# Decays repeated four tiles at a time, row terms of stage 4 beside its values, and another order of turns

## What is computed

```python
x = _layernorm(x + _L0_attn_ref(x, ...))   # stage 0: state space mixer and MLP
x = _layernorm(x + _L0_ffn_ref(x, ...))    # stage 1: attention and experts
x = _layernorm(x + _L1_attn_ref(x, ...))   # stage 2: linear attention
x = _layernorm(x + _L1_ffn_ref(x, ...))    # stage 3: binarized MLP
x = _layernorm(x + _L2_attn_ref(x, ...))   # stage 4: attention, 16 heads, full width
x = _layernorm(x + _L2_ffn_ref(x, ...))    # stage 5: experts
x = _layernorm(x + _L3_attn_ref(x, ...))   # stage 6: attention with pruning
x = _layernorm(x + _L3_ffn_ref(x, ...))    # stage 7: experts
```

```python
delta = softplus(dt @ dt_proj_w.T + dt_proj_b)
dA = exp(delta * A)                       # per token, feature and state
dBu = delta * Bm * u
h = dA_t * h + dBu_t                      # over the 256 tokens; y = sum over states of h * C
```

## Time and profile before

| | before |
|---|---|
| median of 3 runs | 1339.96 us |
| profiled execution: time, span | 1339.95, 1338.2 us |
| mean granted clock of TensorE | 0.978 |
| busy: TensorE, its weight loads | 96%, 68% |
| busy: VectorE, ScalarE, GpSimd | 69%, 68%, 57% |
| chain that ended last: TensorE | 82% |

### The profile page before, as it was taken

How to read it: one execution, slowest core, us unless ns; L and a number is a source line. 1 busy time by engine, 2 the same in 40 slices (tenths; PEclk the granted TensorE clock), 3 DMA queues, 4 the chain that set the end, 5 groups by cost and what they waited for, 6 DMA issues and landing times.

```text
span 1338.2 us, 26178 instructions
## 1 busy us (share of the span) xinstructions
PE 1285.8 (96%) x8764; PEld 910.6 (68%) x8764; DVE 922.5 (69%) x3611; ACT 909.0 (68%) x2503; POOL 768.9 (57%) x845
## 2 busy tenths in 40 slices
PE   8999789999998999999999999999999999999997
PEld 4445356567754777678777777777788877876665
DVE  5777998868757677757566454797597678764244
ACT  6667899777585789675868565557577758755221
POOL 2878877568539477476665755447534525442525
PEclk9679999999998999999999999999999999999999
DMA  8744000110042000102000101201200021004230
GB/s 291 190 127 108 1 2 1 57 57 2 1 142 85 1 2 2 57 24 104 4 1 1 64 1 38 92 1 64 83 2 1 2 80 17 2 1 135 55 103 24
DMA packets 23109, 67.87 MB, mean 51 GB/s; under 512 B 2336, under 2 KB 9120, under 8 KB 20672
## 3 DMA queue, kind: packets, MB, share of 16 engines
q1 hardware_dynamic: 22976, 66.20, 15.6%
HBM read 62.85 MB, written 3.34 MB: 49 GB/s over the span
## 4 chain that ended last, share of the span: by engine, by line
PE 82%; ACT 6%; POOL 5%; DVE 5%; issue 1%; DMA 1%; SPq 0%; POOLq 0%; DVEq 0%; ACTq 0%
PE bank L1193 71%; PE bank L1197 11%; ACT arena L1651 3%; POOL arena L2461 1%; ACT L1651 1%; POOL arena L2465 1%; DVE arena L1912 1%; ACT bank L1651 1%; DVE stats L1926 1%; DVE stats L1915 1%; POOL arena L2524 1%; POOL stats L2452 0%; DVE arena L2091 0%; POOL arena L2474 0%; DVE stats L1929 0%
## 5 line engine op out<-in xcount | busy, mean ns | idle before, releaser
L1651 ACT ACTIVATE arena<-arena 128x256 f32<-128x256 f32 (+4 forms) x804 | 355.8, 446 | 50.1 <-POOL arena L2517 26.5
L1651 ACT ACTIVATE arena<-bank 128x512 f32<-128x512 f32 (+2 forms) x347 | 183.8, 560 | 204.4 <-PE bank L1193 135.1
L1193 PE MATMUL bank<-XT,W 128*128 128x512 f32 (+1 forms) x752 | 293.3, 525 | 0.0
L2474 POOL TENSOR_TENSOR arena<-arena 128x512 f32<-128x512 f32 (+1 forms) x108 | 170.6, 1595 | 153.4 <-DVE arena L1912 50.0
L1193 PEld LDWEIGHTS bank<-W,arena 128*128 128x128 f32 x1888 | 227.9, 192 | 39.2 <-issue 32.0
L1193 PE MATMUL bank<-W,arena 128*128 128x128 f32 x1888 | 238.2, 276 | 1.3 <-DVE arena L2173 0.8
L1193 PE MATMUL bank<-arena 128*32 128x256 f32 (+8 forms) x2912 | 225.5, 334 | 9.8 <-POOL arena L2484 2.7
L2523 POOL TENSOR_TENSOR arena<-arena 128x256 f32<-128x256 f32 x192 | 119.2, 621 | 189.2 <-DVE arena L2163 188.9
L1193 PEld LDWEIGHTS bank<-arena 128*32 128x32 f32 (+4 forms) x2912 | 152.8, 152 | 83.4 <-issue 48.2
L2524 POOL TENSOR_TENSOR arena<-arena 128x512 f32<-128x512 f32 x192 | 201.5, 1049 | 0.0
L1197 PE MATMUL bank<-CF,arena 128*128 128x128 f32 x1312 | 184.0, 277 | 12.0 <-POOL arena L2524 5.3
(11 more groups left out here) (143 smaller groups left out, 1670.2 us busy)
## 6 DMA issues: line engine op xcount, KB each, us to landing
arena<-rws SPq DMA_DIRECT2D x8, 2048.0 KB, 7.5
arena<-rep SPq DMA_DIRECT2D x62, 256.0 KB, 5.3
arena<-rws SPq DMA_DIRECT2D x4, 1792.0 KB, 6.4
W<-w SPq DMA_DIRECT2D x2, 2124.0 KB, 8.2
arena<-rws SPq DMA_DIRECT2D x8, 384.0 KB, 10.1
W<-w SPq DMA_DIRECT2D x1, 2692.0 KB, 9.5
XT<-wkq SPq DMA_DIRECT2D x4, 512.0 KB, 6.0
W<-w SPq DMA_DIRECT2D x1, 2005.0 KB, 15.7
```

The lines of the kernel that those rows point to most:

```text
L1193: return e.matmul(o, lhsT, rhs, start=start, stop=stop, skip_group_check=True)
L1651: return e.activation(o, a, func, **kw)
L2474: e.tensor_tensor(h, h, w, ALU.mult).then_inc(has["gw"], 1)
```

## The change

1. Decays: "0.da" takes four tiles at a time, into banks A, B, C and D, in all four row strips of TensorE. A bank is held until the scan of its tile. The four exponentials of a group follow in one step each, and the condition on the scan of two tiles before is gone.
2. Row terms: the step "4.r" is gone. A new step "4.c" on VectorE copies the row matrix behind the value weights (a place "rk" of 16 columns, loaded as zeros with the weights), so that "4.v" makes values and row terms in one matmul of 144 columns per token tile. It takes two banks, with two tiles each, and VectorE reads values and row terms from both.
3. Costs and turns: the planner's costs are changed in many places (for the load "er" 6.5 in place of 9.0 us, for "ew" 1.5 in place of 2.0), and TURNS is new as a whole. Chunk 1 comes before chunk 0 in stage 0, where chunk 0 came first.

```diff
@@ places and operands
-    [("wv", 128), ("bv", 1), ("wp", 128), ("bp", 128)],
+    [("wv", 128), ("rk", 16), ("bv", 1), ("wp", 128), ("bp", 128)],
-W_AT = {3: WMAX - 1160, 2: WMAX, 4: 4135}
+W_AT = {3: WMAX - 1160, 2: WMAX, 4: 4119}
+        def values4():
+            return W[0][:, W_AT[4]:W_AT[4] + 144]
@@ banks and conditions of the decays
-for _q in range(16):
-    if _q % 2 == 0:
-        HELD["0.da", _q] = [("A", 0, ("0.st", _q, 0), 1, 1), ("B", 0, ("0.st", _q + 1, 0), 1, 1)]
+for _q in range(0, 16, 4):
+    HELD["0.da", _q] = [("ABCD"[_k], 0, ("0.st", _q + _k, 0), 1, 1) for _k in range(4)]
-            if q % 2:
+            if q % 4:
                 add("0.da", q, ("0.da", q - 1))
             else:
-                add("0.da", q, ("0.dc", 0), ("0.a", 0, PREP), *([("0.st", q - 2)] if q >= 2 else []))
+                add("0.da", q, ("0.dc", 0), ("0.a", 0, PREP))
@@ TensorE, 0.da
-                    two = [uses["AB"[k] if name == "0.da" else "bc"[k], name, c, n] for k in range(2)]
-                    for b in two:
+                    some = [uses[k, name, c, n] for k in ("ABCD" if name == "0.da" else "bc")]
+                    for b in some:
                         on.wait_ge(*free(b))
-                    for k, b in enumerate(two):
+                    for k, b in enumerate(some):
                         r, w = slice(32 * (n % 4 + k), 32 * (n % 4 + k) + 32), n // 4 * 128
...
@@ TensorE, 4.v and 4.r
-                    b, ps = first(name, c)
-                    for j in range(4):
-                        ins = mm(ps[:, j * 128:(j + 1) * 128], cols_(4, c)[:, j * 128:(j + 1) * 128], wt(4, "wv"))
-                    ins.then_inc(full[b.i], 1)
+                    on.wait_ge(*after("rk", "4.c", PREP))
+                    for k, (b, ps) in enumerate((first(name, c), second(name, c))):
+                        for j in range(2):
+                            js = slice((2 * k + j) * 128, (2 * k + j + 1) * 128)
+                            ins = mm(ps[:, j * 144:(j + 1) * 144], cols_(4, c)[:, js], values4())
+                        ins.then_inc(full[b.i], 1)
-                elif name == "4.r":
-                    b, ps = first(name, c)
...
-                    for j in range(4):
-                        ins = mm(ps[:, j * 16:(j + 1) * 16], cols_(4, c)[:, j * 128:(j + 1) * 128], pre[:, 48:64])
-                    ins.then_inc(full[b.i], 1)
@@ VectorE, 4.c and 4.v
+                elif name == "4.c":
...
+                    e.tensor_copy(wt(4, "rk"), pre[:, 48:64]).then_inc(has["rk"], 1)
...
+                    for k in range(2):
+                        b = u("bc"[k], name, c)
+                        on.wait_ge(*filled(b))
+                        for j in range(2):
+                            e.tensor_copy(values_in(4, c, 2 * k + j), values_from(bank[b.i][:, 144 * j:144 * j + 128], 0))
+                        tt(row4(c)[:, 32 * k:32 * k + 32].rearrange("p (i h) -> p i h", i=2),
+                           bank[b.i][:, 0:288].rearrange("p (i x) -> p i x", i=2)[:, :, 128:144],
+                           pre[:, 64:80].unsqueeze(1).to_broadcast([128, 2, 16]), ALU.add).then_inc(done[b.i], 1)
```

More of the change, by code:

```diff
@@ L174, in emits @@
     if name == "0.da":
-        return {"dA": (1 - n % 2, 1)}
+        return {"dA": (n % 4 == 0, 1)}
     return EMITS.get(name, {})
@@ L180, in parts_of @@
     t = PARTS[name]
-    t = t[n % 2] if isinstance(t, tuple) else t
+    t = t[n % len(t)] if isinstance(t, tuple) else t
     both = [x.split("|") for x in t.split()]
@@ L311, in stage_steps @@
         add("4.vz")
-        add("4.v", 0, ("4.vz", 0))
-        add("4.r", 0, ("load", 0, PREP, 4))
+        add("4.v", 0, ("4.vz", 0), ("4.c", 0, PREP))
         for i in range(16):
             add("4.qk", i, ("load", 0, PREP, 4), *([("4.ex", last_reader(i - 5))] if i >= 5 else []))
-        attention(lambda u: [("4.r", 0)] + [("4.qk", u // 2 * 4 + k) for k in range(4)], lambda u: [("4.v", 0)])
+        attention(lambda u: [("4.v", 0)] + [("4.qk", u // 2 * 4 + k) for k in range(4)], lambda u: [("4.v", 0)])
         add("4.y", 0, *[("4.pv", u) for u in range(UNITS)])
@@ L359, in weight_steps @@
     return loads + [("0.a", 0, 0, []), ("0.f", 0, 0, []), ("0.w", 0, 0, []), ("3.p", 3, 0, [("1.n", 0, 0, 1)]), ("3.p", 3, 1, [("3.p", 0)]), ("6.a", 6, 0, [("load", 0)])] + [
-        ("1.a", 1, 0, [("0.dt", 0, 0, 0)]), ("3.b", 3, 0, [("1.n", 0, 0, 1)]), ("4.b", 4, 0, [("load", 0)]), ("6.b2", 6, 0, [("load", 0)])]
+        ("1.a", 1, 0, [("0.dt", 0, 0, 0)]), ("3.b", 3, 0, [("1.n", 0, 0, 1)]), ("4.b", 4, 0, [("load", 0)]), ("4.c", 4, 0, [("load", 0)]), ("6.b2", 6, 0, [("load", 0)])]
 TASKS = [[(s, 0) for s in range(8)], [(s, 1) for s in range(8)],
@@ L369 @@
 TURNS = {
[33 rows of a table removed]
-        1352), ("0.e", 0, 3): (1356, 1362, 1366, 1370), ("0.w", 0, PREP): (5,), ("0.f", 0, PREP): (7, 11), ("0.a", 0, PREP): (8,
-        21, 23), ("4.l", 0, PREP): (65, 94, 224, 202), ("4.k", 0, PREP): (114,), ("4.a", 0, PREP): (136, 159, 119, 128, 257, 269,
-        222, 232), ("4.g", 0, PREP): (178, 184, 147, 171, 284, 297, 237, 252), ("4.st", 0, PREP): (194, 186, 343, 301), ("1.n", 1,
[50 rows of a table removed]
-        1841, 1847, 1850, 1855), ("1.a", 1, PREP): (81, 86, 87), ("2.t", 2, 0): (983, 988, 993, 989, 994, 1007, 1034, 1041, 1046,
[22 rows of a table removed]
-        2046, 2049, 2052, 2056), ("3.p", 3, PREP): (387, 404, 413, 420, 432, 439, 448, 489), ("3.b", 3, PREP): (416, 417), ("4.r",
[47 rows of a table removed]
-        (2553, 2556, 2559, 2560, 2562), ("load", 4, PREP): (1252,), ("4.b", 4, PREP): (1313, 1363), ("5.r", 5, 0): (1934, 1941,
[15 rows of a table removed]
-        5, PREP): (1860,), ("6.p", 6, 0): (2619, 2622, 2616, 2620), ("6.qk", 6, 0): (2621, 2650, 2653, 2625, 2636, 2639, 2792,
[53 rows of a table removed]
-        3631, 3634, 3638, -3642), ("load", 6, PREP): (2563,), ("6.a", 6, PREP): (2593,), ("6.b2", 6, PREP): (2707, 2714), ("7.r",
[21 rows of a table removed]
-        3906, 3907), ("load", 7, PREP): (2878,)}
[32 rows of a table added]
+        3): (1381, 1384), ("0.e", 0, 3): (1387, 1390, 1395, 1397), ("0.w", 0, PREP): (6,), ("0.f", 0, PREP): (7, 13), ("0.a", 0,
+        PREP): (10, 12, 14), ("4.l", 0, PREP): (143, 242, 342, 311), ("4.k", 0, PREP): (191,), ("4.a", 0, PREP): (246, 272, 256,
+        265, 360, 384, 350, 362), ("4.g", 0, PREP): (275, 295, 284, 291, 388, 426, 371, 375), ("4.st", 0, PREP): (302, 294, 430,
[50 rows of a table added]
+        ("1.a", 1, PREP): (155, 161, 163), ("2.t", 2, 0): (1135, 1139, 1151, 1147, 1153, 1158, 1183, 1187, 1200, 1195, 1203,
[22 rows of a table added]
+        1977, 1980, 1986, -1989), ("3.p", 3, PREP): (509, 519, 537, 544, 614, 633, 651, 661), ("3.b", 3, PREP): (510, 526),
[46 rows of a table added]
+        (2521, 2524), ("f", 4, 3): (2525, 2528, 2531, 2534, -2538), ("load", 4, PREP): (1298,), ("4.c", 4, PREP): (1342,), ("4.b",
+        4, PREP): (1354, 1358), ("5.r", 5, 0): (1981, 1996, 2002, 2019), ("5.wt", 5, 0): (2042, 2079), ("ew", 5, 0): (2083,),
[14 rows of a table added]
+        3): (2897,), ("f", 5, 3): (2898, 2903, 2906, 2910, -2913), ("load", 5, PREP): (1786,), ("6.x", 6, 0): (2584,), ("6.p", 6,
[53 rows of a table added]
+        6, 3): (3609,), ("f", 6, 3): (3610, 3614, 3617, 3622, -3625), ("load", 6, PREP): (2539,), ("6.a", 6, PREP): (2559,),
+        ("6.b2", 6, PREP): (2568, 2572), ("7.r", 7, 0): (3659, 3663, 3668, 3669), ("7.up", 7, 0): (3667, 3672, 3673, 3679, 3681,
[20 rows of a table added]
+        3): (3880,), ("g", 7, 3): (3881, 3883, 3884), ("load", 7, PREP): (2917,)}
@@ L711, in order_of_steps @@
             if tiled(x) != tiles:
-                more = 0.16 if t < free[g] + 0.1 else 0.09
+                more = (0.0 if tiles == "q" else 0.095) if t < free[g] + 0.1 else 0.09
             elif t > free[g] + 0.1:
@@ L891, in decays0 @@
         def decays0(c, q):
-            return uses["AB"[q % 2], "0.da", c, q - q % 2]
+            return uses["ABCD"[q % 4], "0.da", c, q - q % 4]
         def by_pe(c, q):
@@ L1563, in _ @@
                         ins = mm(ps[:, js], pair(n, 1)[:, js], pair(n, 0)[:, js])
-                    ins.then_inc(full[b.i], 1)
-                elif name == "4.r":
-                    b, ps = first(name, c)
-                    for k in range(4):
-                        on.wait_ge(*emptied(u("b", "4.a", PREP, k)))
-                    for j in range(4):
-                        ins = mm(ps[:, j * 16:(j + 1) * 16], cols_(4, c)[:, j * 128:(j + 1) * 128], pre[:, 48:64])
                     ins.then_inc(full[b.i], 1)
@@ L2294, in _ @@
                     on.wait_ge(*emptied(b))
+                elif name == "4.c":
+                    for k in range(4):
+                        on.wait_ge(*emptied(u("b", "4.a", PREP, k)))
+                    e.tensor_copy(wt(4, "rk"), pre[:, 48:64]).then_inc(has["rk"], 1)
                 elif name == "4.v":
-                    b = u("b", name, c)
```

(17 more changed lines are left out.)

## The result

The changed kernel takes 1358.07 us (median of 4 runs, 1356.59 to 1358.85), the kernel before 1341.29 in the same session: 1.0121 times as long, interval 1.010 to 1.0142. The forecast of 1327 had the wrong sign, and its range ended at 1342.

A forecast was written before the change was run, and what follows sets the result against it. TensorE was taken as the bound from 450 to 1300 us, all engines coupled before 260. 1339.95 - 13 (start) - 4.1 (chunk 3's quads) - 2 (tables) - 2.8 (row terms) + 8.9 (stage 7) = 1326.95, so 1327; range 1312 to 1342.

The forecast's parts named there:

- The rest of the order I take as neutral: Order of turns outside the priced terms: no effect, since between 450 and 1300 us the old order leaves nothing to win.
- chunk 3's quads: Decays of chunk 3: four-tile groups at 1.085 us replace eight pairs at 1.06, 4.1 us less.
- the tables: ScalarE's table switches, mainly around chunk 3's scans: 82 loads instead of 94, 2 us less, ends 0 and 5.
- I take half, 13 us: Before 260 us: TensorE's work falls by 25.1 us, half of it becomes time, 13 us less, ends 0 and 25.
- Stage 7: Gated products of chunks 2 and 3 lose cover by other TensorE steps: 8.9 us more, ends 0 and 12.
- Decays: All four chunks: 16 quads of 1.085 us replace 32 pairs, 21.3 us of TensorE time less, 17.2 in the first three.
- Row terms: Stage 4: the 16-column group goes and value matmuls grow to 144 columns, 2.8 us of TensorE time less.
- Lower clock: Stage 4's weight products 4.a and 4.g move later, to full clock if it is up there: 7.9 us of TensorE less.
- Rival C: Quads hold four of eight banks, so TensorE's queue waits: +8 us, 1348; chance 0.11.
- fewer than 13: Sign of being right: TensorE waits on scans before 260 us fewer than 13 times.
- the sign given for C: TensorE's idle time behind the scans before 260 us grows from 33 us, which would say quads wait for banks.

The follow-up runs named there:

- the old tail: Changed kernel, with the order of the kernel before from turn 3600 on (about the last 130 us, all stage 7): 1345.5 us, ratio 1.000 to 1.004.
- a kernel of their own: Kernel before with only the row terms put beside the values, 4.v taking the places of 4.r: 1342.6 us, ratio 1.000 to 1.002.
- quads in the old order: Kernel before with quads alone in its own order of turns, each second pair's TensorE turn dropped: 1356.8 us, ratio 1.007 to 1.014.
- pairs in the new one: Changed kernel in its new order of turns, with pairs of decays in place of quads: 1369.7 us, ratio 1.015 to 1.025.
- eleven pauses: Changed kernel with the last 130 us in the order before, idle matmuls in eleven TensorE pauses: 1335.3 us, ratio 0.994 to 0.998.
- eight others: Kernel before with idle 128x128 matmuls in eight TensorE pauses between 142 and 363 us: 1340.0 us, ratio 0.999 to 1.001.

## Why the prediction was wrong, point by point

Two steps of the prediction failed. "The rest of the order I take as neutral", with 6.1 us less for chunk 3's quads and the tables: by the account below, the stretch from 300 to 550 us cost 10.3 us more, 16.4 off. And "I take half, 13 us" for the start: 3.3 us less, 9.7 off. Stage 7 was forecast as a loss and is one; the change is slower than the kernel before mainly by it, since with the old tail the two are level. What the forecast counted on to outweigh it, 21.9 us in all, didn't come as time.

- **Decays**: 1.085 us a quad. Measured 1.07 (94.24 to 95.31) at full clock and 2.03 (105.23 to 107.26) at half, and the strips ran side by side. Right. The 21.3 us counted five pairs at their time at half clock as if that part went with the pairs; at full clock the quads save 32 x 1.06 - 16 x 1.07 = 16.8, 4.5 less.
- **Table loads**: 82, as counted. Of the 2 us taken for them nothing shows: from 400 to 450 us TensorE is without work for 7.9 us, before it was 5.3, and the wait of 2.26 us on which the term leaned was released by GpSimd. No run has the table loads alone.
- **Row terms**: about 0.8 us in each chunk where TensorE is the limit (0.7 taken), right; as a kernel of their own they gave nothing in the old order. Chunk 0's 4.r was covered there, so the term should have been at most 3 x 0.8 = 2.4, and "the copy waits for the weights, as the value matmuls do anyway" left out that TensorE would wait for the copy: 4.35 us in that run, none in the changed kernel.
- **Lower clock**: the step that took 7.9 us off for moving 4.a and 4.g was wrong. One 4.a ran at 1.95 us, the next at 3.57 behind a wait of 1.96 us for a scan. Before 300 us the loss is 21.0 us before and 21.8 after. The step took the lower clock for a property of the place. Here the slow 4.a stands behind its pause of 1.96 us, and a quad at 75.96 takes 2.09 us behind one of 6.09: the pauses moved along, and the lower clock with them.
- **The start**: "I take half" of 25.1 us. From the table: 12 quads save 12.6 us, pauses take 8.5 and the clock 0.8 of it, so 3.3 remain of the 13 predicted. I had asked only whether the other engines can use a faster TensorE, and not what a quad does to TensorE's own queue. Rival C named that, but both sides of its sum were off. Its present waits of 20.8 us are 5.9 us of matmuls and 14.9 us of weight loads, which run beside other matmuls or beside those waits; TensorE stood for the 5.9 alone. Its 54 us to come are 29.6 of matmuls with quads in the old order and 16.1 in the changed kernel. Waits of both kinds before 260 us are 20 there, where fewer than 13 was the sign of being right. TensorE's time without work before 260 us grew from 32.6 to 38.4, the sign given for C. C had 0.11. But in the changed kernel quads aren't the whole of it: up to 300 us pauses and loss are 54.2 us before, 75.0 with quads in the old order, 65.9 with pairs in the new one (whose turns weren't searched for) and 63.5 with both. I had put order and quads in one guess.
- **"Rest of the order neutral"**: the largest failure. I looked for room to win between 450 and 1300 us, and none to lose. Between 300 and 550 us the changed kernel adds 6.2 us of pauses and 8.3 of clock, less 4.2 of matmuls, where the prediction took 6.1 off. Pauses and loss there are 13.7 us before, 22.6 with the new order and pairs, 23.6 with quads in the old order and 28.2 with both, so each of the two costs some 9 us there. One pause, 3.21 us before a transpose group at 477.83, is a wait for ScalarE that the old order doesn't have.
- **Stage 7**: 8.9 predicted, 9.7 of gaps and 3.8 of clock measured, 12.6 by the run with the old tail (9.5 by its trace). Mechanism and places right, the clock behind the gaps left out.

From 1326.95 to the profiled 1358.85 in the account's terms (work, pauses, loss): start +9.7 (-3.3 for -13), 300 to 550 us +16.4 (-4.2 of matmuls + 14.5, for -6.1), row terms and other work +2.2 (-0.6 for -2.8), 550 to 1200 us -1.4, stage 7 +5.0 (13.9 for 8.9): 31.9 us. The two kernels do somewhat different work between the same times, so the split between neighbouring stretches is good to a few us only. Executions differ too: between 300 and 450 us the loss is 11.1 us in this trace and 6.6 in that of the run with the old tail, with the same order there.

What stays open: how much of the new order's 15 us outside the tail, seen with pairs, is its own, what the planner's new costs do by handing out the banks otherwise, and whether a table exists that has both the new start and the old middle.

## What to carry to other kernels

Count a merged instruction by the resources that it must have all at once: a quad of 1.07 us in place of two pairs of 1.06 cost 15 us in an order made for pairs and gained 11.6 in one made for quads. On an engine that works in strict order, split the profile into work at full clock, pauses and loss at the lower clock before you price an edit; a microsecond of matmuls taken from a stretch with pauses may come back double. Where TensorE must wait and has a free bank, idle matmuls in the pause can pay: 10.1 us in eleven pauses here, but nothing that could be told in eight others, most of them where VectorE and ScalarE were at 88 and 87%.

## What the runs showed of the hardware that I had not expected

A pause of 2.16 us of TensorE was followed by 13.7 us at 1.2 GHz in one kernel and 17.1 us in another, with 24 matmuls of 65 columns directly behind it; in the 13.7 us TensorE was busy for 13.3. With pairs at that place a pause of 0.83 us was followed by 20.5 us. In the kernel before, a pause of 2.26 us was followed by 6.8 us, with a sum over the states, row terms and a further pause of 0.73 us in them. So the length of the pause alone doesn't give the length of the slow stretch. Eight idle matmuls of 128 columns in the pause of 2.16 us kept 2.4 GHz behind it. A copy of 128 x 16 elements on VectorE took 0.168 us in one kernel and 3.63 us in another, where it ended together with three multiplications of GpSimd.

In the old order quads made TensorE's matmuls wait 33.4 us for scans in place of 5.9: a group over four strips needs four banks, and scans of 1.21 us gave them back one by one. The Trainium skill ("TensorEngine Tiling (Array Packing)", Gotcha 1: PSUM Pressure) says that row tiling raises the pressure on PSUM, since the strips write to different banks. These runs agree with it, with those 33.4 us.
